# A new order for GpSimd's and ScalarE's work in the second group, with pair rows, expert pieces and the last store moved

## What is computed

```python
x = x + xattn(_layernorm(x), k, skip, ctx, ctx, 8)
x = x + ffn(_layernorm(x), gate_w, shared_wg, shared_wu, shared_wd, exp_wg, exp_wu, exp_wd)

# xattn: 32 heads h of 8 rows i or j, causal convolution with k[h] along the 512 positions
kv = v[:, h, i] * x2[:, h, j]
y  = irfft(rfft(kv, 1024) * rfft(k, 1024))[..., :512] + kv * bias
out[:, h, j] = sum_i y[:, h, i, j] * x1[:, h, i]

# ffn: 2048 tokens, top 2 of 8 experts by sigmoid scores, weights normed and scaled by 2.5
shared = (silu(x @ swg.T) * (x @ swu.T)) @ swd.T
routed = sum over the two picked e of w_e * ((silu(x @ wg_e.T) * (x @ wu_e.T)) @ wd_e.T)
```

## Time and profile before

| | us |
|---|---|
| runs (3) | 716.16, 719.92, 720.60; median 719.92 |
| profiled execution | 720.12, its span 718.3 |
| PE busy | 659.9 (92% of the span) |
| DVE busy | 445.2 (62%) |
| POOL busy | 354.6 (49%) |
| ACT busy | 309.9 (43%) |
| mean granted clock | 0.97 |

### The profile page before, as it was taken

How to read it: one execution, slowest core, us unless ns; L and a number is a source line. 1 busy time by engine, 2 the same in 40 slices (tenths; PEclk the granted TensorE clock), 3 DMA queues, 4 the chain that set the end, 5 groups by cost and what they waited for, 6 DMA issues and landing times.

```text
span 718.3 us, 11574 instructions
## 1 busy us (share of the span) xinstructions
PE 659.9 (92%) x3475; PEld 332.1 (46%) x3476; DVE 445.2 (62%) x689; ACT 309.9 (43%) x422; POOL 354.6 (49%) x304
## 2 busy tenths in 40 slices
PE   5989878899899999799999998999979999999993
PEld 3534334344344445344444433445535555555551
DVE  5999795798977677987796787774322221222110
ACT  5386677382235464233531276633422333233321
POOL 3899899927757524784566005500242222322232
PEclk8899999999999999989999999999989999999998
DMA  7945236130326500313413668949996888898854
GB/s 208 287 108 135 67 88 134 28 80 23 134 74 145 135 15 16 104 53 55 99 31 119 239 194 291 310 125 244 220 180 107 125 131 128 134 129 131 133 80 58
DMA packets 130521, 91.58 MB, mean 127 GB/s; under 512 B 96993, under 2 KB 110817, under 8 KB 129953
## 3 DMA queue, kind: packets, MB, share of 16 engines
q1 hardware_dynamic: 121728, 71.49, 40.9%
q0 software_dynamic: 8176, 18.75, 14.3%
q10 hardware_dynamic: 576, 0.82, 0.5%
HBM read 46.32 MB, written 25.65 MB: 100 GB/s over the span
## 4 chain that ended last, share of the span: by engine, by line
PE 57%; DVE 13%; POOL 9%; ACT 8%; DMA 6%; issue 4%; SPq 1%; POOLq 0%; ACTq 0%; DVEq 0%
PE banks L830 17%; PE banks L832 17%; PE banks L831 17%; POOL arena L663 6%; DMA out<-xf,ids 4%; POOL arena L691 2%; PE banks L922 2%; PE banks L866 1%; PE banks L927 1%; PE banks L926 1%; POOL arena L730 1%; DVE mixT L1495 1%; DMA arena<-split_filters 1%; DVE arena L1488 1%; DVE hm L1625 1%
## 5 line engine op out<-in xcount | busy, mean ns | idle before, releaser
L663 POOL TENSOR_TENSOR arena<-arena 128x512 f32<-128x512 f32 x120 | 138.9, 1188 | 59.3 <-ACT arena L1186 29.9
L793 POOL DMA_INDIRECT out<-xf,ids x39 | 62.5, 1603 | 185.3 <-DMA out<-xf,ids 123.5
L830 PE MATMUL banks<-arena 128*128 128x512 f16 (+1 forms) x330 | 124.9, 379 | 17.6 <-DVE arena L1488 13.1
L831 PE MATMUL banks<-arena 128*128 128x512 f16 (+1 forms) x330 | 124.8, 378 | 0.0
L832 PE MATMUL banks<-arena 128*128 128x512 f16 (+1 forms) x330 | 124.6, 378 | 0.0
L830 PE MATMUL banks<-arena,normed 128*128 x312 | 98.4, 315 | 5.2 <-issue 5.2
L831 PE MATMUL banks<-arena,normed 128*128 x312 | 98.3, 315 | 0.0
L832 PE MATMUL banks<-arena,normed 128*128 x312 | 98.3, 315 | 0.0
L1842 DVE SCALAR_TENSOR_TENSOR hm<-banks,silu 128x256 f32<-128x256 f32 x39 | 16.5, 424 | 126.0 <-PE banks L832 118.6
L1488 DVE TENSOR_TENSOR arena<-banks,arena 128x512 f32<-128x512 f32 x128 | 80.8, 681 | 14.5 <-PE banks L832 13.8
L1133 ACT ACTIVATE arena<-arena 128x2048 f16<-128x2048 f32 x31 | 59.0, 1904 | 69.9 <-POOL arena L663 67.3
(11 more groups left out here) (205 smaller groups left out, 1096.3 us busy)
## 6 DMA issues: line engine op xcount, KB each, us to landing
arena<-split_filters SPq DMA_DIRECT2D x31, 256.0 KB, 3.4
arena<-in_expert_w SPq DMA_DIRECT2D x12, 544.0 KB, 7.8
stages<-in_expert_w SPq DMA_DIRECT2D x10, 544.0 KB
arena<-in_ctx_hidden SPq DMA_DIRECT2D x4, 1024.0 KB, 7.8
arena<-in_ctx SPq DMA_DIRECT2D x8, 512.0 KB, 6.2
out<-x_tok SPq DMA_DIRECT2D x6, 512.0 KB, 5.2
x_tok<-in_expert_w SPq DMA_DIRECT2D x5, 544.0 KB
mixT<-in_expert_w SPq DMA_DIRECT2D x5, 544.0 KB, 7.3
```

The costliest lines, as they stand in the source:

```text
L663: nc.gpsimd.tensor_tensor(kv[s % 2][:, lb * COLS:(lb + 1) * COLS].rearrange("p (b j i) -> p b j i", i=NH, j=NH), v[:, a, None, :].to_broad ...
L793: nc.gpsimd.indirect_dma_start(out=out, out_offset=bass.IndirectOffsetOnAxis(ap=ids[slot][:, 0:1], axis=0), in_=yg[slot], in_offset=None, ...
L830: nc.tensor.matmul(dst, wh, xh, start=(k == 0), stop=False)
L831: nc.tensor.matmul(dst, wh, xl, start=False, stop=False)
```

## The change

Four edits, in nothing of which the arithmetic or PE's own list changes.

First, in the second group GpSimd and ScalarE get a new order up to the fifth convolution, and DVE finishes the products of each convolution there ahead of the norm's work. Second, `pairs` is split: `pair_ranks` stays, and in the second and third groups `pair_rows` comes one convolution later; its wait for the scatters of the group before moves with it. Third, in the last stage the gating of a block has no expert piece ahead of its high and low part, two expert pieces move behind the pairs and one behind `tile_table`; one load and one piece in the loop over tiles come a tile later. Fourth, SyncE stores the last group's rows by the first tile instead of the second.

```diff
-        loads_behind = {0: (6, 2), 2: (6, 3), 3: (7, 0), 4: (7, 1), 5: (7, 2), 6: (7, 3)}
-        pieces_behind = {1: [(6, 0), (6, 1)], 2: [(6, 2)], 4: [(6, 3)]} | {c + 5: [(7, c)] for c in range(EX_PARTS)}
+        between = {1: [(1, 2), (1, 3)], 2: [(3, 0), (3, 1)], 3: [(3, 2)], 4: [(3, 3)]}
+        loads_behind = {1: (6, 2), 2: (6, 3), 3: (7, 0), 4: (7, 1), 5: (7, 2), 6: (7, 3)}
+        pieces_behind = {1: [(6, 0), (6, 1)], 3: [(6, 2)], 4: [(6, 3)]} | {c + 5: [(7, c)] for c in range(EX_PARTS)}
...
@@ SyncE, loop over the first tiles
-                if t == 1:
+                if t == 0:
                     sp.wait_ge(base_ready, Q * G)
                     store(out_rows[G - 1], x_tok[(G - 1) % 3], base_stored)
...
@@ GpSimd, groups
-                    if g != 1 or h != 3:
+                    if g == 1 and h < 4:
+                        if h == 0:
+                            outer(s0 + 2)
+                            piece(5)
+                            low_parts(s0 + 2)
+                            inverse_root(1)
+                            outer(s0 + 3)
+                            low_parts(s0 + 3)
+                            outer(s0 + 4)
+                            outer(s0 + 5)
+                            low_parts(s0 + 4)
+                            piece(6)
+                            piece(7)
+                        continue
+                    if g != 1 or h > 4:
                         low_parts(s0 + h)
-                    if g == 1 and h == 2:
-                        low_parts(s0 + 3)
...
@@ ScalarE, groups
                     if g == 1 and h == 2:
-                        next_parts(s0 + h + 1)
+                        turn_filter(s0 + h + 1)
                     for i in shared_at.get((g, h), ()):
                         shared(i)
                     if g == 1 and h == 2:
                         load_sigmoid(0)
+                        scores(0)
+                        load_silu(0)
+                        high_parts(s0 + h + 2)
+                        turn_filter(s0 + h + 2)
+                        gated(0, 0)
+                        high_parts(s0 + h + 3)
+                        continue
+                    if g == 1 and h == 3:
                         continue
...
@@ ScalarE, last stage
                 gated_silu(G - 1, m, gates[m % 2])
+                gated_high(G - 1, m)
                 if m < SM - 1:
                     expert(3 + (m - 1) // 2, 2 * (m - 1) % EX_PARTS)
-                gated_high(G - 1, m)
-                if m < SM - 1:
                     expert(3 + (m - 1) // 2, 2 * (m - 1) % EX_PARTS + 1)
...
@@ DVE, pairs
             def pairs(g):
+                pair_ranks(g)
+                pair_rows(g)
+            def pair_ranks(g):
                 t = turn_bank("rank", g, 0)
-                if g > 0:
-                    dve.wait_ge(rows_sent, 16 * 2 * Q * g)
                 dve.wait_ge(rank_ready, g + 1)
...
+            def pair_rows(g):
+                if g > 0:
+                    dve.wait_ge(rows_sent, 16 * 2 * Q * g)
+                dve.wait_ge(rank_used, g + 1)
                 for k in range(2):
...
@@ DVE, start of a group; for g == 1 now
                     products(s0, 0, g)
+                    dve.wait_ge(outT_ready, Q)
+                    total(s0, 0)
                     mixed_tile(0, 2)
                     mixed_tile(0, 3)
                     mixed_moments(0)
                     mixed_moments(0, True)
+                    products(s0 + 1, 1, g)
+                    mixed_shift(0)
+                    total(s0 + 1, 1)
+                    feed_low(0, range(0, 2))
+                    products(s0 + 2, 2, g)
+                    feed_low(0, range(2, Q))
+                    total(s0 + 2, 2)
...
@@ DVE, fifth to eighth convolution of a group
-                    if h == (6 if g < G - 1 else 4):
+                    if g == G - 1 and h == 4:
                         pairs(g - 1)
+                    elif g < G - 1 and h == 6:
+                        pair_ranks(g - 1)
+                    elif g < G - 1 and h == 7:
+                        pair_rows(g - 1)
                     finish(s0 + h, h, g)
...
@@ DVE, last stage
-            gated_product(G - 1, 0, ups[0])
-            expert(1, 2)
-            gated_low(G - 1, 0)
-            expert(1, 3)
+            gated(G - 1, 0, ups[0])
             pairs(G - 1)
             for m in range(1, SM):
                 gated_product(G - 1, m, ups[m % 2])
-                if m < 3:
-                    expert(3, 2 * m - 2)
+                if m < SM - 1:
+                    expert(*between[m][0])
                 gated_low(G - 1, m)
                 if m < 3:
-                    expert(3, 2 * m - 1)
+                    expert(*between[m][1])
```

More of the change, by code:

```diff
@@ L752, in _ @@
                 second_outer(q)
[L753 to L754 removed]
+            pieces_at = {(0, 3): [0], (0, 4): [1], (0, 5): [2], (0, 6): [3], (0, 7): [4], (1, 4): [8]}
             for g in range(G):
@@ L1736, in _ @@
                     mixed(g - 1)
-                if g > 1:
                     add_shared(g - 2, 0)
-                total(s0, 0)
-                if g > 1:
+                    total(s0, 0)
                     add_shared(g - 2, 1)
-                mixed_shift(g - 1)
-                low_parts(s0 + 2)
-                if g > 1:
+                    mixed_shift(g - 1)
+                    low_parts(s0 + 2)
                     feed_low(g - 1)
@@ L1747, in _ @@
                     add_shared(g - 2, 3)
-                if g == 1:
-                    products(s0 + 1, 1, g)
-                    feed_low(0, range(0, 2))
-                    total(s0 + 1, 1)
-                    feed_low(0, range(2, Q))
-                else:
                     finish(s0 + 1, 1, g)
-                low_parts(s0 + 3)
-                finish(s0 + 2, 2, g)
+                    low_parts(s0 + 3)
+                    finish(s0 + 2, 2, g)
                 low_parts(s0 + 4)
```

2 lines of the change are left out of this document (removed).

## The result

The changed kernel takes 743.17 us (median of 4 runs, 741.39 to 744.27) against 718.57 of the kernel before, run beside it: a ratio of 1.0341 [1.0298, 1.0385]. The direction was forecast, the size was not: 24.6 us lost where 10.5 were expected, outside the range.

A forecast was written before the change was run, and what follows sets the result against it. PE is busy 92% of the span, so only its stops and slow clock count. Second group +7.5, third +3.5, last stage −0.5 make +10.5 us: 730.4 us from a 719.92 median; forecast's own range 725 to 736, whole range 716 to 737.

The forecast's parts named there:

- The wait and its chain: Third group: GpSimd waits 10.4 us for late pair rows, then scatters, outer product, silu and gating; PE's down product at 323.0.
- the two stops that vanish: Second and third groups: each pair of short PE stops goes with its slow clock, about 7 and 8.0 us gained.
- +3.5: Third group: PE +2.2 us late at its first down product, +1.3 behind it; bounds +2 and +5.5.
- +7.5: Second group: +4.7 us at and behind the down products, plus 2.8 for the later `outer(17)`; bounds +3.5 and +10.5.
- The scatters, "12.3": GpSimd, from pair rows to the next outer product: 12.3 us, landing 1.83 included, against 14.0 before the change.
- the quiet price: Scatters on GpSimd: four issues undisturbed by DVE take 4.78 us; without this price 1.7 us more at each place.
- I take `outer(17)` 2.8 us later: Second group: late row load and filter 13 delay this outer product by 2.8 us; bounds 0 and 4.5.
- And +1.3 behind it: Behind the first down products: DVE's low part, products and two mixed tiles delay the next transposes by 1.3 us.
- Last stage, "−0.5": Last stage: the 2.46 us stop can go, tile rows may be fetched later; −0.5 us, bounds −4 and +2.
- The first: Rival: second group's first half closes up, silu of block 0 before about 119; 714 us, or 710; chance 0.12.
- The worse case: Rival: pair rows meet busy GpSimd, or scatters stay at 14.0, row load and filter late; +18, 738 us; chance 0.08.
- The first half of the second group: Up to PE's resumption at 128.95: some 7 us stop ahead of convolution 11, nothing gained but the clock, 0 to 1.5 us.

## Why the forecast went wrong

The ledger's 22.45 us against the 10.5 of the sum: 7.4 more in the second group, 0.6 in the third, 4.0 in the last stage.

**The wait and its chain: right, to a tenth of a microsecond in the third group.** From the end of the outer product (306.87) to PE's resumption (336.92) are 30.05 us; the sum had 30.05. The pair rows' own time and the two stops that vanish came as told, and so did the low clock behind the new stops, though not its price. The third group as a whole came to +4.14 against +3.5 because two errors partly cancel: PE was 1.3 us later at its down products, not 2.2, and the slow clock cost 2.85.

**Second group, +14.86 instead of +7.5: three terms mis-sized.** (1) The scatters, "12.3": from pair rows to outer product 18 it took 16.19 us, 3.9 more, in the landing and not in the issues, which kept to 0.96 to 1.19 us. So the quiet price for the issues was right (no run here tells a two-port mode of DVE, on which the prediction leaned, from its other work); but a landing of 1.83 us was carried over to a moment when it shared the DMA engines with a megabyte. That load was in sight, though not among the rows: it follows the total of convolution 15 in the trace of before too, and the scatters were being moved onto it. The run with the load apart shows 3.2 us of this. The Trainium skill (DMA: Bandwidth & Descriptors, section "Queues, rings and completion order") says that each DMA engine takes turns between queue rows, packet by packet; that a scatter of another queue then waits among the megabyte's packets fits these rows, and no run here shows it packet by packet. (2) "I take `outer(17)` 2.8 us later": it was 4.96 (184.18 against 179.22), above the upper bound of 4.5. I had PE's slack absorb a part and found the filter as the cause; the runs show two causes ending 1.2 us apart, filter 13 and outer product 14 behind the shared pieces, and the pieces' effect on the latter was not in the sum at all. (3) "And +1.3 behind it": this stood for DVE's work ahead of the next transposes, for which PE had no stop at all; the slow clock, which the sum put at nothing although PE was said to be "ending cold", cost 2.46 us (and 2.85 in the third group). In the earlier trace rows it had cost 3.0 for a stop of 2.96 us.

**Last stage, "−0.5": +2.4 and +3.2 in two experiments, +3.45 in the trace.** The stop of 2.46 did shrink, to two of 1.17 and 1.00. Counted from the last ranks, PE then reached its last down products 1.7 us sooner, but DVE's low part for them came 1.6 us later, behind the tile table and an expert piece: a stop of 3.33 us, and 2.9 of slow clock. I had followed the fetch of the tile rows, which bound nothing, and not the next gating. Part of the size may be this execution's: from the ranks to the first tile it lost 4.54 us, the eleven other traces with this order 0.9 to 2.6, with stops of 2.60 to 2.65.

**The rivals.** The first fell: the silu of block 0 ran at 128.36, not before 119. The worse case got the direction of the miss, not its cause: pair rows met no busy GpSimd, and its 738 took scatters of 14.0 us, a bound that was too narrow, since it was read where no large load crosses them.

**The first half of the second group** went as worked out: filter 11 let PE go on at 116.47 (forecast 116.4), the silu of block 0 came at 128.36 (128.2), PE resumed at 129.71 (128.95). The stop ahead of convolution 11 was 4.73 us and not 7, since PE came there later: the granted clock in convolution 10 was 0.79 over 8.31 us, behind a stop of 2.75.

## What to carry to other kernels

Work that an in-order engine waits for must not be made later unless everything behind the wait on that engine is costed to its last consumer; a wait of 0.54 us became 10.8 here, and the gain of some 15 us from the short stops that vanished paid for about half of the 29.7 lost at the two long ones and behind them. A transfer moved to a new moment takes the price of that moment: look at what else is issued there. A burst with a landing wait in its middle can be cut there and useful work put in (here worth 12 us with the pair rows in place, 706 against 718.8, and 18 with them late); and where two chains end together, test both edits at once, since one alone can show nothing.

## What the runs showed of the hardware

DVE's short operations beside a running GpSimd were held for about one GpSimd instruction at most in the kernel before (0.8 to 1.2 us for the ones that were held, 8.50 us in all for 2.2 us of pair rows), but twice through nearly a whole run of eight: 7.51 us for an operation that takes 0.17, and 8.55 us for one that takes 0.69. Two more of the first kind took 3.30 and 3.98 us (the runs with scatters behind the outer product and with the silu ahead). All three of the first kind ended 0.03 to 0.04 us after GpSimd's low parts did, ahead of its next outer product. With GpSimd held back the first took 0.17 again. The Trainium skill (SBUF — State Buffer, section "SBUF: two separate sides") has the port that DVE and GpSimd share locked for one instruction at a time; by that a wait ends at the next of GpSimd's 1.03 us instructions, and these rows show it going on through several. Why it does so at some places and not at others, and whether it makes the spread of 10 us between runs of one kernel, stays open.
